# A planner's ranks given chunk by chunk, its times measured anew, and the copies of turned probabilities moved to ScalarE

## The reference, cut to what matters

```
x = layernorm(x + scan0(x))        # 256 channels x 32 states
x = layernorm(x + ffn(x))          # silu(gate) * up, hidden 704
x = layernorm(x + mamba(x))        # conv of 4 taps, 512 channels x 16 states, gate, projection
x = layernorm(x + moe_block(x))    # below

h = dA * h + dBu                   # one step of a scan: for every token, channel and state
y = sum over states of h * C

h = rmsnorm(x) * ln1_w             # moe_block: 16 heads of 128, causal over its tokens
attn = softmax(q @ k.T / sqrt(128) + mask)
x = x + (attn @ v) @ wo
t = rmsnorm(x) * ln2_w             # 16 experts, the best 6 kept, and one shared expert
out = x + routed(t) + shared(t)
```

## Time and profile before

| | us |
|---|---|
| median of 3 runs | 1346.62 (1346.56 to 1347.63) |
| profiled execution, its own time | 1343.95 |
| its span, first to last instruction | 1342.6 |
| TensorE busy | 1120.5 (83%) |
| VectorE busy | 994.4 (74%) |
| GpSimd busy | 635.8 (47%) |
| ScalarE busy | 605.5 (45%) |
| mean granted TensorE clock | 0.928 of 2.4 GHz |

### The profile page before, as it was taken

How to read it: one execution, slowest core, us unless ns; L and a number is a source line. 1 busy time by engine, 2 the same in 40 slices (tenths; PEclk the granted TensorE clock), 3 DMA queues, 4 the chain that set the end, 5 groups by cost and what they waited for, 6 DMA issues and landing times. The chain is left out here.

```text
span 1342.6 us, 17016 instructions
## 1 busy us (share of the span) xinstructions
PE 1120.5 (83%) x5224; PEld 879.7 (66%) x5224; DVE 994.4 (74%) x1829; ACT 605.5 (45%) x1561; POOL 635.8 (47%) x521
## 2 busy tenths in 40 slices
PE   4757346598796889987977899799999999999897
PEld 2535224476685677765756787578787877777676
DVE  5988999889898788899998865699945444444433
ACT  5554555456564435455753323566542123333210
POOL 3776588964665887645776840276610000000000
PEclk9778768799798999997989999899999999999899
DMA  3773135343365865333676641265544543331263
GB/s 110 252 235 84 48 111 141 112 129 97 96 184 166 227 212 174 113 119 116 204 222 169 211 130 36 90 205 192 177 138 131 180 137 106 106 106 59 83 193 102
DMA packets 105435, 191.55 MB, mean 143 GB/s; under 512 B 11648, under 2 KB 42368, under 8 KB 105088
## 3 DMA queue, kind: packets, MB, share of 16 engines
q1 hardware_dynamic: 91520, 177.42, 42.9%
q10 hardware_dynamic: 13824, 13.05, 2.9%
HBM read 176.33 MB, written 14.09 MB: 142 GB/s over the span
## 5 line engine op out<-in xcount | busy, mean ns | idle before, releaser
L1976 DVE TENSOR_TENSOR_SCAN scan_banks<-scan_banks,h_end,drive 128x256 f32<-128x256 f32 x480 | 337.2, 743 | 16.3 <-POOL drive L2295 13.3
L2339 POOL TENSOR_TENSOR sum<-sum,state 128x512 f32<-128x512 f32 x174 | 221.5, 1273 | 67.1 <-DVE state L1988 64.3
L2295 POOL TENSOR_TENSOR drive<-w0T,bc_rows 128x512 f32<-128x512 f32 x128 | 163.8, 1288 | 70.4 <-DVE scan_banks L1976 56.2
L2295 POOL TENSOR_TENSOR drive<-w1T,bc_rows 128x512 f32<-128x512 f32 x128 | 162.7, 1278 | 59.9 <-DVE scan_banks L1976 46.2
L2342 POOL TENSOR_TENSOR stats_b<-stats_b,neg_half 128x2 f32<-128x2 f32 x12 | 8.3, 694 | 351.5 <-DVE stats_b L2140 183.8
L1988 DVE TENSOR_TENSOR state<-scan_banks,bc_rows 128x512 f32<-128x512 f32 x240 | 163.1, 679 | 1.3
L1420 PE MATMUL score_banks<-state,ident 128*128 128x256 f32 x256 | 86.6, 491 | 70.8 <-DVE state L1988 49.0
L1398 PE MATMUL work_bank<-hT,streamed_w 128*128 128x256 f32 x548 | 134.4, 387 | 3.5 <-DVE x L2178 3.1
L1595 PE MATMUL work_bank<-probsT,kv 128*128 128x256 f32 (+1 forms) x532 | 129.0, 366 | 6.8 <-ACT probsT L1895 4.7
L1420 PEld LDWEIGHTS score_banks<-state,ident 128*128 128x128 f32 x256 | 58.6, 243 | 98.8 <-DVE state L1988 59.8
L1712 ACT ACTIVATE scan_banks<-delta0T,a 128x256 f32<-128x256 f32 x256 | 110.6, 470 | 16.0 <-DVE state L1988 12.0
(11 more groups left out here) (208 smaller groups left out, 2121.7 us busy)
## 6 DMA issues: line engine op xcount, KB each, us to landing
bc_rows<-bc_rows SPq DMA_DIRECT2D x256, 256.0 KB, 3.5
streamed_w<-in_w_head SPq DMA_DIRECT2D x64, 384.0 KB, 5.0
expert_w<-in_w_moe SPq DMA_DIRECT2D x52, 384.0 KB, 4.3
kv_past<-kv ACTq DMA_DIRECT2D x48, 256.0 KB, 3.9
kv<-in_w_moe SPq DMA_DIRECT2D x32, 384.0 KB, 4.0
kv<-kv_past SPq DMA_DIRECT2D x16, 768.0 KB, 4.7
kv<-kv_past SPq DMA_DIRECT2D x16, 512.0 KB, 5.2
streamed_w<-in_w_moe SPq DMA_DIRECT2D x16, 384.0 KB, 3.9
```

The costliest lines, as they stand in the source:

```text
L1976: done = e.engine.tensor_tensor_scan(states, decays, drive[g % len(drive)][:, i, 0:size], h_end[layer][:, n, kt:kt + 1], ALU.mult, ALU.add)
L2295: self.tt(drive[g % len(drive)][:, :, 0:size], w_of(layer, c)[:, PAIR * half:PAIR * (half + 1), 0:size], rows_of(g, c, 0), ALU.mult).then_ ...
L2339: self.tt(to, so_far, slot_of(c, layer, k), ALU.add).then_inc(added, 1)
```

## The change

1. **Ranks.** Each lane's bonus becomes a tuple in a table `RANKS`: one number per chunk (per chunk and layer for the lanes of scan units). `Lane.bonus(stage)` looks it up. The factors `EARLIER` are new too.
2. **Planned times.** The durations of most stages are changed, the default `lag` goes from 0.2 to 0, the 0.15 after a part becomes a number per engine (`SEEN`), and TensorE's planned durations are stretched by 22%, 9.5%, 5.5% and 2% up to the planned times 262, 500, 750 and 1000 (`PE_PACE`).
3. **Copies.** `on_scalar` gives ScalarE all copies of chunks 0 and 1, and j = 0 and 2 of chunk 2. Chunk 3 stays as it was.

No instruction is added or removed. 64 stages of copies go from VectorE to ScalarE and 16 (j = 1 of chunk 2) the other way, and all five queues get a new order. Everything else (tiles, buffers, banks available, arithmetic) is the same. Which bank a stage takes, and which instruction follows which, is the planner's result.

```diff
-def pe(*columns):
-    return "pe", sum(0.012 + 0.00169 * n for n in columns)
+def pe(*columns):
+    return "pe", sum(0.004 + 0.00167 * n for n in columns)
...
-    return "dve", sum(0.155 + 0.00104 * n for n in widths)
+    return "dve", sum(0.102 + 0.00106 * n for n in widths)
...
-    return "act", sum(0.16 + 0.00086 * n for n in widths)
+    return "act", sum(0.13 + 0.00086 * n for n in widths)
...
+RANKS = {
+    "fetches": (2.7, 2.7, 2.6, 2.7, 2.95, 2.95, 2.7, 2.4),
...
+    "hidden": (2.7, 2.95, 1.8, 1.95),
...
+    def bonus(self, stage):
+        return self.ranks[self.rank_of(*stage.run.args)]
...
-                Lane(self.hidden(), 1.60, 6),
+                Lane("hidden", self.hidden(), 6),
...
-            move = act(pairs * P) if on_scalar(c, j) else dve(pairs * P)
+            move = (act if on_scalar(c, j) else dve)(*[hi - lo for lo, hi in spans(c, j)])
...
-EARLIER = {'pe': 0.3, 'dve': 0.1, 'act': 0.7, 'pool': 1.0, 'sp': 1.0}
+EARLIER = {'pe': 0.2, 'dve': 0.0, 'act': 0.6, 'pool': 0.0, 'sp': 1.3}
+PE_PACE = (262, 1.22), (500, 1.095), (750, 1.055), (1000, 1.02)
+SEEN = {'pe': 0.2, 'dve': 0.12, 'act': 0.12, 'pool': 0.12, 'sp': 0.0}
...
-                key = (start - lane.bonus * EARLIER[engine], -lane.bonus, ready)
+                bonus = lane.bonus(stage)
+                key = (start - bonus * EARLIER[engine], -bonus, ready)
...
+        if engine == "pe":
+            us *= next((slower for until, slower in PE_PACE if start < until), 1.0)
         over = start + us
         clock[engine] = over
-        lane.emitted(entry, over + 0.15)
+        seen = over + SEEN[engine]
+        lane.emitted(entry, seen)
...
-    return j == 2 if c == LAST else j % 2 == 1
+    return j == 2 if c == LAST else c < 2 or j != 1
```

More of the change, by code:

```diff
@@ L236, with rank_at, unit_at, __init__ @@
 TABLE = 1.3
+RANKS = {
+    "fetches": (2.7, 2.7, 2.6, 2.7, 2.95, 2.95, 2.7, 2.4),
+    "decays": (-0.2, 2.95, 1.4, 0.1, 0.5, 0.8, 0.4, -0.95),
+    "drives": (-0.0, -0.6, 0.8, -0.5, 1.35, 0.65, 1.35, 3.0),
+    "scans": (-1.25, -1.35, -1.25, -0.9, -0.25, -1.1, -0.7, -0.1),
+    "weighs": (2.1, 1.75, 1.3, 1.05, 2.15, -0.4, 0.45, -0.9),
+    "carries": (2.0, 2.05, 1.25, 2.2, 2.1, 2.45, 2.2, 2.65),
+    "adds": (-1.35, -0.75, -1.35, -0.1, 2.0, 1.25, 2.4, 2.55),
+    "skips": (2.5, -0.25, 1.15, 2.85, 1.6, 2.6, 1.3, 0.5),
+    "first": (0.4, -1.4, -1.1, -1.15),
+    "second": (2.45, 1.9, 2.0, 2.7),
+    "into_heads": (2.2, -0.05, 1.45, -0.5),
+    "projections": (1.4, 1.2, 1.0, 0.05),
+    "scores": (1.55, 1.55, 2.5, 0.1),
+    "products": (1.1, 1.6, 1.3, 0.4),
+    "results": (2.0, 2.4, 2.55, 0.5),
+    "experts": (2.35, 1.75, 1.7, 2.55),
+    "routing": (3.0, 2.7, 3.0, 3.0),
+    "weights": (0.55, 0.5, 0.85, 1.4),
+    "hidden": (2.7, 2.95, 1.8, 1.95),
+    "weighed": (2.7, 2.25, 2.7, 2.7),
+    "sums": (0.5, 2.35, 0.75, 3.0),
+    "load_lane": (-0.35,),
+    "chore_lane": (2.6,),
+}
+def rank_at(c=0, *_):
+    return c
+def unit_at(_, c, layer, *__):
+    return layer * CHUNKS + c
+RANKED_BY = {"load_lane": lambda *_: 0, "chore_lane": lambda *_: 0, "scans": lambda _, *unit: unit_at(*unit),
+             "skips": lambda c, half=None: c if half is None else CHUNKS + c}
+RANKED_BY |= dict.fromkeys(("fetches", "decays", "drives", "weighs", "carries", "adds"), unit_at)
 class Lane:
-    def __init__(self, stages, bonus=0.0, window=12):
-        self.stages, self.bonus, self.window = stages, bonus, window
+    def __init__(self, name, stages, window=12):
+        self.ranks, self.rank_of = RANKS[name], RANKED_BY.get(name, rank_at)
+        self.stages, self.window = stages, window
         self.queue, self.over = deque(), False
+    def bonus(self, stage):
+        return self.ranks[self.rank_of(*stage.run.args)]
     def candidates(self):
@@ L356, in scans @@
             for i in range(PAIR):
[L357 removed]
+                yield Stage(partial(self.p.scan, i, g, c, layer, k), (("dve", 0.052 + 0.00246 * SIZES[c]),), after, (("scan", g),) if i else ())
     def weighs(self):
@@ L754, in weave @@
     units = Units(p, reached)
-    lanes = [*Chain(p).lanes(), Lane(load_lane(p), 1.0), Lane(chore_lane(p), -0.90), *units.lanes(), *Attention(p).lanes()]
+    lanes = [*Chain(p).lanes(), Lane("load_lane", load_lane(p)), Lane("chore_lane", chore_lane(p)), *units.lanes(), *Attention(p).lanes()]
     def places(stage):
```

66 lines of the change are left out of this document (33 added, 33 removed).

## The result

The changed kernel takes **1305.9 us** in the median of 4 runs (1303.27 to 1307.65), the kernel before 1347.12 beside it: ratio 0.9688, 95% interval 0.9665 to 0.9711. It is 3.1% faster. The forecast was 1329 with a range from 1311 to 1352: the sign is right, the size is not, and the time lies under the range.

What follows compares the result with a forecast made beforehand. VectorE's queue was taken to bound the kernel up to chunk 2's output, TensorE after 772 us. The moves alone gave 1353.6; less 28.3 of saved idle time, 1325.3, with overheads 1329 us, range 1311 to 1352.

Steps and rivals of the forecast that it cites:

- Chunk 0's output, +6.3: VectorE up to chunk 0's third norm: three more scan units of chunk 1 go ahead, all on the path, 6.3 us later.
- Stretch 0 to 1, -9.7: VectorE between outputs of chunks 0 and 1: copies and expert multiplications leave, some scan work is added, 9.7 us shorter.
- Stretch 1 to 2, -38.9: VectorE between outputs of chunks 1 and 2: copies, scans, weighings, expert multiplications and ranking leave, 38.9 us shorter.
- TensorE's third stretch: TensorE from chunk 2's first V projection to chunk 3's: 52.9 us of moved expert work gives 263.0 busy; idle 12.9 halved.
- The last stretch, 0: TensorE from chunk 3's first V projection to the end: the same work in either order, so no change.
- ScalarE at nothing: ScalarE takes over copies, in all about 30 us, counted as 0 because its own idle time covers them.
- the sign of being wrong: TensorE's products with V (line 1595) waiting more than 15 us in all on ScalarE's copies would show the forecast wrong.
- The rival of ScalarE's queue: Copies stand behind saved states in ScalarE's queue and come late: 20 us, 1349; chance 0.19 together with TensorE starving.
- the 9.7 us that I took whole: VectorE's waits for TensorE inside or at the end of expert blocks (7.2 and 2.5 us), all expected to go.
- The quarter: VectorE's other 48.7 us of idle time between outputs of chunks 0 and 2: a quarter, 12.2, expected to go.
- the third rival: VectorE between 256 and 718 us runs at 5% idle, all TensorE's 12.9 us goes too: 1307; chance 0.17.
- The starving rival: TensorE starves early and is late at the end, VectorE's idle time stays: 1357.7; chance 0.19 together with ScalarE's queue.

Runs made afterwards that it cites:

- vector_load: The changed kernel, same order, with unread reductions added to VectorE beside the score reductions, about the size of the copies that left: 1309.44 us.
- copies_only: The kernel before with only the new rule for which copies ScalarE takes, ranks and planned times old: 1369.23 us, ratio 1.0178.
- experts_late: The kernel before with chunk 1's gate and up projections planned after chunk 2's first V projection: 1394.8 us, ratio 1.0367.
- flat_refit: The changed kernel with one rank per lane for all chunks, these ranks and `EARLIER` picked anew for a short plan: 1327.57 us, ratio 0.9867.
- copies_back_refit: The changed kernel with the old rule for the copies and eight rank numbers picked anew for it: 1324.14 us, ratio 0.9845.

## Why the prediction was wrong in size

Step by step, by its own numbers:

- *Chunk 0's output, +6.3.* The units are there (VectorE is busy 223.7 us up to it, 218.8 before, +4.9), but the output comes at 254.0, and 255.1 before. VectorE's idle time up to it fell from 36.2 to 30.3. "VectorE idles little there" rested on the stretch from 174; ahead of it VectorE had 32.1 us of idle time (21.7 us up to 91, and 10.4 from there to 174), which the prediction left out, and has 24.6 now. 7.4 us of error.
- *Stretch 0 to 1, -9.7.* VectorE's busy time fell by 1.5 (208.55 against 210.06). Copies, gates and scans are as counted. Some 8 us above the count come from operations that are as many as before and took longer here: 2.8 of them belong to the softplus groups of the last section.
- *Stretch 1 to 2, -38.9.* Measured -39.3. Right.
- *TensorE's third stretch, 263.0 busy with 6.5 idle.* Measured 260.8 with 6.2. Right, and so is the account behind it: what left the second stretch is in the third.
- *The last stretch, 0.* It is 2 us shorter, 346 against 348.
- *ScalarE at nothing.* Right in the trace. Its copies and who waits for them, the first two lines from the waits of TensorE, the others from those of ScalarE:

```profile
PE work_bank L1454 <- ACT probsT L1951: 4.9, 2, 4.4
PE work_bank L1651 <- ACT probsT L1951: 3.4, 1, 3.4
```
```profile
ACT h_end L1781 <- DVE state L2044: 101.0, 84, 8.4
ACT probsT L1951 <- PE work_bank L1460: 37.0, 28, 2.8
```

TensorE waits for them 8.3 us in 3 waits, of which 3.4 are before products with V, where the sign of being wrong was 15, and ScalarE still waits for TensorE. The rival of ScalarE's queue did not come about. A copy of 512 columns takes 596 ns on ScalarE and 677 on VectorE:

```profile
L1951 ACT ACTIVATE probsT<-work_bank 128x512 f32<-128x512 f32 x40 | 23.9, 596 | 20.9 <-PE work_bank L1651 13.6 <-PE work_bank L1460 5.8 <-PE scan_banks L1651 0.7
```
```profile
L2220 DVE COPY probsT<-work_bank 128x512 f32<-128x512 f32 x30 | 20.3, 677 | 15.6 <-PE work_bank L1460 15.6
```

So the row was right to go by. The Trainium skill's advice ("ScalarE: Activation LUTs", rules for kernel authors) to give simple elementwise work to VectorE, which it bases on bf16, is no guide for these copies in float32 out of PSUM.

**The step that failed** is the sentence on idle time: "Of the other 48.7 [...] I take a quarter, 12.2", with the 28.3 us in all that it led to. Against the sum with all idle time staying, 1353.6, the span is 51.6 us shorter:

| | taken | measured |
|---|---|---|
| up to chunk 2's output (717.7 by the sum, 681.5 measured) | 21.9 | 36.2 |
| from it to the V projection (12.4, now 7.8) | 0 | 4.6 |
| TensorE's third stretch (275.9, now 267.4) | 6.4 | 8.5 |
| the last stretch | 0 | 2.2 |

Of the 36.2, 7.4 are from before chunk 0's output, and 28.8 from the two stretches, where the idle time fell by 36.1, in place of 21.9, and the busy time was 7.7 above the count (0.4 is the rounding of the window ends). By waits: the 9.7 us that I took whole did go, but with the like of them the fall is from 11.0 to 3.9, and of all other idle time some 29 us went, where I took 12.2. The quarter had no row behind it. The third stretch's idle time fell by 6.7, as taken (6.4). What the trace did offer was the stretch 174 to 256 at 5% idle, and the third rival built on it: 4.3% and 6.1% idle now, 1303 by its sum for a span of 1302.0. It was given 0.17 because there were no heads in that stretch; with heads it ran as well. Its idle time for VectorE was right; that its sum meets the end within 1 us is luck, since it took all of TensorE's 12.9, of which 6.2 stayed, and left out the 7.7 us of longer work and the gains before chunk 0's output, at the V projection and at the end. Beside that rival stood the Trainium skill's rule of the most-contended engine ("Perfetto Trace Analysis", identifying the most-contended engine), by which the copies would come off whole, 1313. The time is near that, but the mechanism isn't: vector_load put 32.7 us back and lost 5, and copies_only took them off alone and lost 24. The Trainium skill's next section in "Perfetto Trace Analysis" (optimization strategy) says that performance may be improved by interleaving regimes whose most-contended engine differs. That is nearer to this case, where chunk 1's expert block was moved from VectorE's regime into TensorE's, but no rule either: the same move alone lost 49 us.

One reading of the prediction was loose: VectorE does not fall to 4 tenths from slice 27 on, where TensorE's 9s begin, but from slice 30. In slices 27 to 29 both stand at 9. No term of the sum rests on it.

The starving rival has its mechanism shown by experts_late (49 us) and didn't come about in the change. Which of the two it would be depended on the plan as a whole, and nothing in the trace of before could settle it. The one thing that could have told was the plan's own end, 1347.4 against 1278.2: with all error of 9 to 32 us in it, it would have given 1287 to 1310. But that spread is known only from the runs made here.

Of the signs named ahead, three came: chunk 1's expert block behind chunk 2's output, VectorE's idle time under 45 us, and TensorE at 9 tenths (8 in two slices, 7 in the last) behind it. The times for chunk 0's, 1's and 2's outputs (258 to 263, near 487, 690 to 708) and for chunk 3's V projection (near 980) were all too late, by 4, 15, 9 and 23 us, counted from the near end of each range.

**What the parts are worth** can be said only against fitted plans: the ranks by chunk some 24 us (0.9867 against 0.9688), the copies on ScalarE some 21 (0.9845 against 0.9688). These are estimates from one fitted plan each, and upper bounds if flat_refit and copies_back_refit were searched less than the change; for copies_back_refit only eight numbers were picked anew. The new times gain nothing alone, but the fitted plans are made with them. What they are worth by themselves stays open: ranks fitted with the old times weren't run. (Given the old times with the change's ranks and copies, the planner finds no order: it stops at about 217 us of its clock with work left over.)

**Open.** Why the copies give some 21 us after a fit where VectorE's load costs 5: the places where they stand may matter (a turned piece copied by an idle ScalarE may free its PSUM bank sooner than one in VectorE's full queue), but no run separates that. Nor is it shown what makes the plan early by 9 us in one order and 32 in another.

## What to carry to other kernels

Where one order is picked at the minimum of a search, taking one part back measures mostly the distance from that minimum: here 0.1 of noise on every rank cost 18 and 31 us, about as much as most parts did. Before a cost is put down to a part, perturb the tuned numbers with nothing taken away, and fit the rest again. And when a change re-plans an order as a whole, a fraction of the idle time that no row supports is a weak term: here the best stretch that the kernel already showed (5% idle) was nearer to what came (4.3% and 6.1%), and deserved more weight.

## What was not expected of the hardware

Some of VectorE's operations took over twice as long in one place as in another. The row of the softplus sum, before and then after, by form:

```profile
L2039 DVE TENSOR_TENSOR delta0T<-sT,hiddenT 128x512 f32<-128x512 f32 x4 | 2.8, 691 | 0.1
```
```profile
L2095 DVE TENSOR_TENSOR delta0T<-sT,hiddenT 128x512 f32<-128x512 f32 x4 | 4.7, 1164 | 0.1
```

The same operation on the same tiles: 691 ns each before, 1164 in the mean after. The timeline of the changed kernel, VectorE at 16.6 and 77.8 us and GpSimd at 77.2, shows where:

```profile
16.58 0.69 DVE L2095 TENSOR_TENSOR delta0T<-sT,hiddenT 128x512 f32<-128x512 f32 x1
```
```profile
77.80 1.64 DVE L2095 TENSOR_TENSOR delta0T<-sT,hiddenT 128x512 f32<-128x512 f32 x1
```
```profile
77.16 1.73 POOL L2351 TENSOR_TENSOR drive<-w0T,bc_rows 128x512 f32<-128x512 f32 x1 [2.00 <-DMA bc_rows<-bc_rows]
```

With GpSimd idle it takes 0.69 us; at 77.8 it runs into a `drive` of GpSimd and takes 1.64, and the `drive` takes 1.73, where the mean of its kind is 1.30. Both its inputs lie in SBUF. The weighing, of the same size, reads one input from PSUM, stands beside GpSimd's work in the whole scan regime, and stays at 676 ns (679 before). The Trainium skill has this rule ("SBUF — State Buffer", who interferes with whom): VectorE contends with a GpSimd instruction that reads SBUF when both its own inputs are there, and not with one input. The trace agrees, and both lose time. Three such groups (lines 2086, 2088 and 2095 after; 2030, 2032 and 2039 before) have means of 1347, 1086 and 1164 ns where they had 1228, 771 and 691: 12 x 0.12 + 12 x 0.32 + 4 x 0.47 = 7 us on VectorE in the whole span that no count of instructions shows. That more such pairs meet because both engines idle less is my reading, and no run separates it. Either way this price was missing from the sum.
